# The mask for the step size's logarithm is written by ScalarE instead of VectorE

## What is computed

```
xs  = silu(causal_conv(x @ W_in))
dbc = xs @ W_xproj                       # dt_in, Bm, Cm
dt  = softplus(dt_in @ W_dt + b_dt)      # the step size
dA  = exp(dt[..., None] * A)             # A = -exp(A_log), 16 states
dBx = dt[..., None] * Bm * xs[..., None]
h   = scan(h[t] = dA[t] * h[t-1] + dBx[t])
y   = einsum(h, Cm) + D * xs
y   = y * silu(z); out = y @ W_out
```

## Time and profile before

| | |
|---|---|
| runs | 7480.49, 7483.51, 7493.04 us |
| the profiled execution | 7491.75 us |
| its span, first to last instruction | 7489.9 us |
| mean granted TensorE clock | 0.952 of full speed |
| instructions | 112318 |
| main loop and its lead-in | about 190 to 6990 us of the span |
| DMA, mean | 138 GB/s, 37% of 16 engines for the main queue |

### The profile page before, as it was taken

The page is one execution under the profiler, slowest core; times in us unless marked ns, Lnnn a source line. Parts: engine busy times, 40 slices in busy tenths (PEclk is TensorE's granted clock), DMA queues, the critical chain, the costliest instruction groups (busy, mean ns, idle before and its releaser), DMA issues. The chain is left out here.

```text
span 7489.9 us, 112318 instructions
## 1 busy us (share of the span) xinstructions
PE 6585.2 (88%) x33290; PEld 3740.9 (50%) x33290; DVE 6636.6 (89%) x8221; ACT 6174.7 (82%) x13680; POOL 870.9 (12%) x555
## 2 busy tenths in 40 slices
PE   6888888899999999999999999999999999998571
PEld 3444444455555555555555555555555555554240
DVE  2788989899999999999999999999999999999844
ACT  5777777788888889888898888988898888888435
POOL 0053635320000000000000000000000000000075
PEclk8998999999999999999999999999999999999775
DMA  3343433343334333333334333343333333343367
GB/s 107 114 145 130 148 114 128 109 148 135 137 133 153 140 135 139 136 148 144 132 135 147 148 135 137 138 147 142 139 139 131 146 141 132 133 152 131 134 124 226
DMA packets 282207, 1035.92 MB, mean 138 GB/s; under 512 B 37570, under 2 KB 129526, under 8 KB 273824
## 3 DMA queue, kind: packets, MB, share of 16 engines
q1 hardware_dynamic: 248352, 1014.00, 37.0%
q0 software_dynamic: 33792, 21.18, 1.8%
HBM read 955.77 MB, written 90.98 MB: 140 GB/s over the span
## 5 line engine op out<-in xcount | busy, mean ns | idle before, releaser
L880 DVE TENSOR_TENSOR_SCAN hs<-dA,hs 128x1584 f32<-128x1584 f32 x512 | 1766.4, 3450 | 3.1 <-ACT dA L690 2.9
L613 ACT ACTIVATE P<-psS,least_s 99x197 f32<-99x197 f32 x4096 | 1495.9, 475 | 153.4 <-DVE least_s L819 153.4
L1114 PE MATMUL psS<-KM,Q 128*99 128x394 f32 x4096 | 1559.6, 504 | 8.4 <-ACT PTs L621 4.2
L690 ACT ACTIVATE dA<-dt_,aneg 128x394 f32<-128x394 f32 x2048 | 1238.9, 642 | 212.2 <-DVE hs L880 192.6
L819 DVE TENSOR_REDUCE least_s<-psS 99x2 f32<-99x394 f32 x2048 | 1083.9, 561 | 120.2 <-PE psS L1114 99.2
L1121 PEld LDWEIGHTS psS<-cst,P 99*99 99x99 f32 x8192 | 849.9, 166 | 464.9 <-ACT P L613 396.0
L1121 PE MATMUL psS<-cst,P 99*99 99x99 f32 x8192 | 988.6, 257 | 67.9 <-ACT P L613 56.8
L621 ACT ACTIVATE PTs<-psS 99x396 f32<-99x396 f32 x2048 | 983.6, 552 | 40.5 <-PE psS L1121 31.5
L871 DVE TENSOR_TENSOR hs<-hs,u 128x1584 f32<-128x1584 f32 x512 | 922.0, 1801 | 63.4 <-DMA hs<-bc_scratch 63.4
L885 DVE TENSOR_TENSOR hs<-hs,cr 128x1584 f32<-128x1584 f32 x512 | 922.7, 1802 | 10.0
L1114 PEld LDWEIGHTS psS<-KM,Q 128*99 128x99 f32 x4096 | 600.0, 165 | 522.4 <-issue 324.3
(11 more groups left out here) (221 smaller groups left out, 9288.4 us busy)
## 6 DMA issues: line engine op xcount, KB each, us to landing
hs<-bc_scratch SPq DMA_DIRECT2D x512, 792.0 KB, 5.9
cr<-bc_scratch SPq DMA_DIRECT2D x512, 792.0 KB, 4.3
pat<-patches SPq DMA_DIRECT2D x64, 1176.0 KB, 6.8
more_scratch<-zeros SPq DMA_DIRECT2D x64, 197.0 KB, 3.2
rows_scratch<-hs SPq DMA_DIRECT2D x1, 12352.0 KB, 43.0
PTs<-more_scratch SPq DMA_DIRECT2D x24, 512.0 KB, 7.1
sum_scratch<-HW SPq DMA_DIRECT2D x64, 148.5 KB
hs<-rows_scratch SPq DMA_DIRECT2D x24, 386.0 KB, 3.4
```

The lines of the kernel that those rows point to most:

```text
L613: last = nc.scalar.activation(P[:, r, b, m, 0:T], psS[0:CT, 2 * r + b, m * T:(m + 1) * T], ACT.Exp, bias=least_s[:, r, b, m:m + 1], scale= ...
L690: last = nc.scalar.activation(shifted(dA[:, g % 2, k, :]), images(dt_[:, d, :]), ACT.Exp, scale=aneg[:, d, n:n + 1])
L880: nc.vector.tensor_tensor_scan(h, a, h, 0.0, ALU.mult, ALU.add).then_inc(scan_ready, 1)
L1114: mm(psS[0:CT, 2 * r + b, 0:2 * T].rearrange("p (e t) -> p e t", e=2), Q[:, r, b, q * CT:(q + 1) * CT], KM[:, r, h % 2 * 2:h % 2 * 2 + 2, ...
```

## The change

ACT writes the mask itself. It computes the positive part of 2^-8 - sp, which is above zero just where sp < 2^-8, into `small`, now a float tile. DVE's comparison and its wait for sp are gone, and the copy by mask reads the same bits as whole numbers. The constant 2^-8 needs a column of its own in `epsr`, a bias for ACT. The new instruction stands between the square and the logarithm. The hand-written orders of the units are as before.

```diff
-        epsr = sb("epsr", [128, 3])
+        epsr = sb("epsr", [128, 4])
...
-        small = sb("small", [128, N], mybir.dt.uint32)
+        small = sb("small", [128, N])
...
-            nc.gpsimd.memset(epsr[:, 2:3], -(3 ** 0.5) / 4).then_inc(pool_ready, 1)
+            nc.gpsimd.memset(epsr[:, 2:3], -(3 ** 0.5) / 4)
+            nc.gpsimd.memset(epsr[:, 3:4], LOG1P_SERIES).then_inc(pool_ready, 1)
...
                 nc.scalar.activation(shifted(u[:, d, :]), images(sp[:, :]), ACT.Square, bias=epsr[:, 2:3], scale=3 ** -0.5).then_inc(poly_ready, 1)
+                nc.scalar.activation(small[:, :], sp[:, :], ACT.Relu, bias=epsr[:, 3:4], scale=-1.0)
                 nc.scalar.activation(spl[:, :], sp[:, :], ACT.Ln, bias=1.0).then_inc(sp_ready, 1)
...
             def step_size(i, d):
                 k = i * 2 + d + 1
-                dve.wait_ge(spe_ready, k)
-                nc.vector.tensor_scalar(small[:, :], sp[:, :], LOG1P_SERIES, None, ALU.is_lt)
                 dve.wait_ge(poly_ready, k)
                 back(nc.vector.scalar_tensor_tensor(out=shifted(u[:, d, :]), in0=shifted(u[:, d, :]), scalar=13 / 16, in1=images(sp[:, :]), op0=ALU.add, op1=ALU.mult), i)
                 dve.wait_ge(sp_ready, k)
                 dve.sem_inc(dve_waited, 1)
-                back(nc.vector.copy_predicated(images(spl[:, :]), images(small[:, :]), shifted(u[:, d, :])), i)
+                back(nc.vector.copy_predicated(images(spl[:, :]), images(small[:, :]).bitcast(mybir.dt.uint32), shifted(u[:, d, :])), i)
```

## The result

The changed kernel takes 7506.09 us, the median of 15 runs, against 7488.03 us for the kernel before in 15 runs beside them: a ratio of 1.0025, 95% interval 1.0016 to 1.0034. That is 18 us slower, at the edge of what can be told from no change. It lies inside the predicted range (7466 to 7512) and above the likeliest case's own range (7475 to 7500). One of the 15 executions took 11237 us at a mean granted clock of 0.58, and the ratio leaves it out. The profiled execution after took 7499.92 us, span 7498.1.

A forecast was written before the change was run, and what follows sets the result against it. The prediction took DVE as nearly full, PE close behind, and ACT as setting the time around direction 0. It added 27 us for direction 0 and took off 26 for half-clock stretches: 7486 us, range 7466 to 7512.

The forecast's parts named there:

- the likeliest case: Whole kernel: direction 0's cost of +27 us and about -26 from fewer half-clock stretches; range 7475 to 7500 us, chance 0.55.
- DVE's saving is covered: Direction 0: the 0.27 us that DVE gains by losing the comparison becomes a wait there.
- Direction 0 costs what it occupies on ACT: ACT's unbroken stretch in direction 0: the new instruction's 0.42 us passes through PE to DVE, 27 us (20 to 34).
- Direction 1 is absorbed: Direction 1: ACT's delay of up to 0.42 us vanishes in DVE's waits for rs and a DMA; costs and earns nothing.
- Fewer half-clock stretches: 51 iterations after routing: about 12 stretches near 76 us instead of 27, with late ones some 16 iterations.
- Given back: 52.5 - 26 = 26 us: 51 iterations: half-clock stretches cost 52.5 us before and 26 after the change, so 26 us return.
- Sum: Whole kernel: 7491.75 + 27 - 26 = about 7493 for the profiled execution; from the four executions' average of 7487, 7486.
- rival 1: PE's half-clock stretches stay as many, all 27 near 76 us: slower, 7513 us; chance 0.18.
- Rival 3: Nearly all half-clock stretches go, the last broken up by moved idle time: faster, 7463 us; chance 0.14.
- the late stretches: Five half-clock stretches 93.4 to 94.2 us after H, where PE idles ahead of up's matmuls; left at 4, 5 us.
- Rival 4: ACT's idle time hides the new instruction in both directions, same runs of stretches: 7486 us, no change; chance 0.05.

The follow-up runs named there:

- with the constant: Changed kernel with scale and bias of the new ACT instruction as numbers, no bias read from a tile: 7506.67 us, ratio 1.0028.
- the two kernels that kept its full-clock length: Changed kernel with ACT's mask for direction 1 only, DVE comparing for direction 0: 7480.26 us; changed kernel with no mask made: 7508.47 us.
- both fillers: Extra PE matmuls in idle time ahead of wo and up, added to the kernel before (7439.49 us) and to the changed one (7474.58 us).
- direction 0 alone: Changed kernel with ACT writing the mask for direction 0 only, DVE comparing for direction 1: 7521.08 us, ratio 1.0045.

## Why the prediction was right, and where it was short

*DVE's saving is covered.* Right. 0.27 us is gained at the polynomial and waited away 4.6 us later; without any mask the iteration still lasts 104.03.

*Direction 0 costs what it occupies on ACT.* The path was right: it alone makes 0.54 us, a second instruction there 0.45 more, and nothing is given back at 3481.18. The size was wrong, and it is the mis-sized term: 0.42 us x 64 = 27 was forecast, and 0.51 was occupied and 0.48 to 0.58 passed on, 31 to 37 us. Between the occupied time and what is passed on the profiles can't tell a difference. I had taken the logarithm as the nearest row and put the square's 0.53 down to its output in two pieces. What counted was the bias: the new instruction reads it from a tile, as the square does, and the logarithm does not. Two rows of the kernel before could have told it, of equal shape and both read from PSUM, with an operand from a tile and without (busy us and mean ns in all, then idle time before); their medians are 592 and 499 ns, 93 apart:

```profile
L649 ACT ACTIVATE XZ<-psB,vec 128x394 f32<-128x394 f32 x128 | 76.5, 598 | 61.3 <-PE psB L1186 61.3
L649 ACT ACTIVATE XZ<-psB 128x394 f32<-128x394 f32 x128 | 67.5, 527 | 1.8 <-PE psB L1182 1.8
```

The Trainium skill (ScalarE: Activation LUTs, What ACT_TABLE_LOAD costs) gives an instruction with constants 186 ns and 0.833 ns per element, about 93 ns more for each operand per partition, and an overlap of about 93 ns with the next; that would be an estimated 607 ns here and 514 from start to start. The trace agrees: 610 ns, 0.51 us; 515 ns and 0.42 us with the constant. The prediction had gone by another section of that page.

*Direction 1 is absorbed.* Right within what the runs tell. In the aligned pair, counted from H and less direction 0's 0.51 us, the copy by mask came 0.18 us later (forecast: 0 to 0.1), Hn 0.50 later (forecast: 0.41) and hs by u 0.08. The copy's wait of 0.47 us for the logarithm is the 0.18 that it had before and the 0.27 that DVE gained. The cover at rs and at the DMA took the rest. What the prediction did not have is the DVE idle time of some 4 us, once, in the last iteration of the 51.

*Fewer half-clock stretches.* Right in kind: 12 and 14 of 51 for the forecast's 16, mostly single, in iterations of 106.3 us, and near 76.5 us. The weak step is the sum over it, "Given back: 52.5 - 26 = 26 us", which takes its 52.5 from one profile. In the profiled pair the 51 iterations gave back all but 0.8 of the 29.6 us that 0.58 us each cost. So for that pair the term was right. But the profile of the kernel before had the higher of the counts known for it: in its repeat it had 21, in the two kernels that kept its full-clock length 23 and 25. The 51 iterations take 54 and 34 us more than 51 times their profile's full-clock length in the two profiles of the kernel before, and 25 and 28 us more in the two of the changed one (6 and 4 us of that in the last iteration), so between 6 and 29 us are given back, by which profiles are compared, and 17 or 18 in the mean. And the ten routed iterations ahead, which the prediction did not treat apart, gave back nothing.

*Sum.* With the price of 35 us from the kernels with both fillers, 17 are given back if the medians are to come out at +18; the forecast had +27 and -26. The two errors point the same way. That they make up the miss is bookkeeping, since the 17 is the difference of 35 and 18, but the two profiles of each kernel have about the same. They put the cost elsewhere, though: in the mean the changed kernel's 51 iterations are 9.5 us longer and its lead-in 15.5, where 11 iterations of 0.48 to 0.58 us are about 6. The forecast also took 7486 us for the changed kernel and for the kernel before in its rivals; its own sum of +27 and -26 on 7487 is 7488. That the measured time lies in the predicted range owes something to the width of that range, which reaches into rival 1: the likeliest case's own range missed it by 6 us. Rival 1 had named this side (7513), but not for its reason: the stretches did become fewer. Its point of decision, more than 22 of 51, was not reached. Rival 3's breaking up of the late stretches did happen, worth some 5 us (3 to 5 late ones at 1.2 to 1.4 us). Rival 4, ACT's idle time, falls with direction 0 alone.

That the stretches come from a match between the iteration's length and their own return is supported by three lengths, not proven. At 103.93 to 104.03 us 21 to 32 iterations of 51 have one, in rows of up to 11 near 76 us, 105.8 us apart. At 104.46 to 104.56 us 12 to 17 have one, and the commonest distance is 419.8 us, four iterations (3 x 104.56 + 106.26 = 419.9). At 105.01 us 19 have one, and the commonest distance is 211.6 us, two iterations (105.01 + 106.71 = 211.7). With PE at work in the idle place near 76 us there are none. So 105.8 us is not the only return; what sets these distances is not worked out here, and a longer iteration does not always have fewer.

A mask on GpSimd was not tried, nor the new instruction at a place of ACT's list with idle time behind it.

## What to carry to other kernels

Where several nearly full engines go in step, an instruction is worth what it costs on the engine that has no idle time between it and the next hand-over: moved there from a covered place it costs in full, and the saving on the other becomes a wait. Take its price from start to start, from a row with the same kinds of operands as well as the same shape; a bias from a tile alone is 0.09 us of ACT here (610 against 515 ns). Where the total also holds a part that comes and goes with the clock, compare iterations at full clock first, then count the others, and do both in more than one execution: full-clock iterations of one kernel differed by 0.1 us between two.

## What the runs showed of the hardware that I had not expected

- A few matmuls of no use, put at two places where PE would sit idle, made the kernel 0.66% faster (7439.49 against 7490.51 us): TensorE kept 2.4 GHz in all 51 iterations, where it had fallen to 1.2 GHz for 3.4 us in 21 to 32 of them. 29 of the 51 us came with the second place.
- The number of these stretches fell when the iteration became longer: from 21 to 32 in 51 at 103.98 us to 12 to 14 at 104.46 to 104.56 us, and rose to 19 at 105.01. A slower iteration can look cheaper than it is for this reason.
- In the last of the 51 iterations DVE stands idle for 3.96 to 5.38 us, released by nothing that the trace shows, in every kernel whose DVE work was changed, and never in the kernel before, with fillers or without. The iteration lasts 107.80 to 110.72 us there, and 103.77 to 104.25 in the kernel before. The cause is open.
